# One GNN kernel on one core: the fixed one-hots read a kept column and stand ahead of the list load

## The reference

```python
x = _layernorm(x + _L0_gnn_ref(x, edge_index, ...))                # three SAGE layers
x = _layernorm(x + _L1_gnn_ref(x, edge_index, edge_attr_16, ...))  # one GIN layer with edge features
x = _layernorm(x + _L2_gnn_ref(x, edge_index, edge_weight, ...))   # two GCN layers
x = _layernorm(x + _L3_gnn_ref(x, ..., src, dst, edge_type_8))     # two RGCN layers, 8 relations
```

## Time and profile before

| | |
|---|---|
| three runs | 5378.65, 5391.27, 5395.21 us; median 5391.27 us |
| profiled execution | span 5394.1 us; no other time of it is given |
| PE busy | 4403.8 us, 82% |
| DVE busy | 3418.7 us, 63% |
| ACT busy | 2417.1 us, 45% |
| POOL busy | 1920.8 us, 36% |
| DMA | 815.61 MB, mean 151 GB/s |

### The profile page before, as it was taken

The page is one execution under the profiler, slowest core; times in us unless marked ns, Lnnn a source line. Parts: engine busy times, 40 slices in busy tenths (PEclk is TensorE's granted clock), DMA queues, the critical chain, the costliest instruction groups (busy, mean ns, idle before and its releaser), DMA issues.

```text
span 5394.1 us, 129622 instructions
## 1 busy us (share of the span) xinstructions
PE 4403.8 (82%) x25128; PEld 2883.3 (53%) x25129; DVE 3418.7 (63%) x10510; ACT 2417.1 (45%) x4969; POOL 1920.8 (36%) x1886
## 2 busy tenths in 40 slices
PE   6998997767878888867777588887799996888895
PEld 4664554333445555435554355544577773667772
DVE  5553454676545555448997688876466663777774
ACT  2442442554357777626664466664222221333332
POOL 5650782654033433116550434310433312333310
PEclk9999999898889999989999899998899999999998
DMA  4663884555334444326563466653444433444332
GB/s 142 217 210 116 267 270 142 182 182 176 99 117 148 146 151 145 113 88 174 174 172 105 143 203 212 203 177 108 145 136 136 136 120 103 133 122 133 116 111 76
DMA packets 443919, 815.61 MB, mean 151 GB/s; under 512 B 70872, under 2 KB 76818, under 8 KB 443828
## 3 DMA queue, kind: packets, MB, share of 16 engines
q1 hardware_dynamic: 389172, 697.28, 38.6%
q0 software_dynamic: 54656, 117.32, 9.1%
HBM read 480.10 MB, written 334.22 MB: 151 GB/s over the span
## 4 chain that ended last, share of the span: by engine, by line
PE 46%; issue 14%; DVE 12%; ACT 8%; DVEq 6%; POOL 5%; DMA 4%; ACTq 3%; SPq 1%; POOLq 0%
PE p_agg L1116 7%; PE p_edge L1103 7%; PE p_agg L1118 6%; PE p_tr L1103 6%; PE p_agg L1149 5%; POOL raw L680 4%; DVE onehot L1550 4%; DMA h_in<-feature 3%; DVE stats L1640 3%; ACT o L881 2%; ACT u L900 2%; PE p_wide L1236 2%; PE p_agg L1142 2%; PE p_dense L1192 2%; PE p_dense L1168 2%
## 5 line engine op out<-in xcount | busy, mean ns | idle before, releaser
L1550 DVE TENSOR_SCALAR onehot<-iota,dst_f,negbase 128x512 f16<-128x512 f16 (+1 forms) x2848 | 1110.7, 444 | 823.8 <-PE p_agg L1149 304.8
L1116 PE MATMUL p_agg<-onehot,msg 128*128 128x512 f16 (+1 forms) x2848 | 1135.9, 399 | 584.9 <-DVE onehot L1550 325.1
L680 POOL DMA_INDIRECT raw<-node_s,src_i x980 | 958.1, 978 | 1462.8 <-DMA node_s<-o 560.6
L1118 PE MATMUL p_agg<-onehot,msg 128*128 128x512 f16 (+1 forms) x2848 | 1135.7, 399 | 0.0
L1116 PEld LDWEIGHTS p_agg<-onehot,msg 128*128 x2848 | 281.7, 99 | 930.7 <-issue 780.8
L680 POOL DMA_INDIRECT raw<-node_x,src_i x392 | 378.2, 965 | 553.3 <-DMA feature<-more_masked 253.7
L1149 PE MATMUL p_agg<-h_in,w 128*128 128x512 f32 x784 | 442.5, 648 | 110.6 <-DMA h_in<-feature 109.4
L881 ACT ACTIVATE o<-v_ring,nmr,rstd 128x128 f32 (+1 forms) x1176 | 472.3, 483 | 60.0 <-DVE nmr L1656 55.3
L1640 DVE BATCH_NORM_STATS2 stats<-v_ring 128x6 f32 (+1 forms) x1960 | 417.5, 278 | 44.1 <-DVE v_ring L1630 14.7
L900 ACT ACTIVATE u<-v_ring,nmr,rstd 128x128 f32 (+1 forms) x784 | 312.4, 481 | 223.9 <-DVE res_in L1686 135.6
L1118 PEld LDWEIGHTS p_agg<-onehot,msg 128*128 x2848 | 282.9, 99 | 218.9 <-issue 33.1
(11 more groups left out here) (260 smaller groups left out, 7817.8 us busy)
## 6 DMA issues: line engine op xcount, KB each, us to landing
node_s<-o SPq DMA_DIRECT2D x392, 256.0 KB
h_in<-feature SPq DMA_DIRECT2D x392, 256.0 KB
feature<-u SPq DMA_DIRECT2D x294, 256.0 KB
node_x<-o SPq DMA_DIRECT2D x294, 256.0 KB
res_in<-node_x SPq DMA_DIRECT2D x294, 256.0 KB
h_in<-node_s SPq DMA_DIRECT2D x196, 256.0 KB
h_t<-dinv_scratch SPq DMA_DIRECT2D x196, 256.0 KB, 3.6
h_in<-in_x SPq DMA_DIRECT2D x98, 256.0 KB
```

The source lines that it names most:

```text
L680: nc.gpsimd.indirect_dma_start(out=raw[:, (e % RING) * BATCH + j, :], out_offset=None, in_=src_d, in_offset=bass.IndirectOffsetOnAxis(ap=s ...
L1116: nc.tensor.matmul(p_agg[:, a, :], tile_ap(msg, t, 0, D), oh, start=first, stop=True, skip_group_check=True)
L1118: return nc.tensor.matmul(p_agg[:, a, :], tile_ap(msg, t, D, 2 * D), oh, start=False, stop=True, skip_group_check=True)
L1550: return V.tensor_scalar(tile_ap(onehot, slot), iota[:, :], dst_f[:, bass.ds(t, 1)], negbase[:, bass.ds(it * 2 + a, 1)], ALU.subtract, ALU ...
```

## The change

Three things change, all in DVE's program.

1. A new SBUF tensor `place` of 128 x 294 f32 (98 halves x 3). In round 0, behind the three fixed compares of a half, DVE adds the tiles' `dst_f` columns and the half's `negbase` column into it. In the seven rounds after, `fixed_onehots` compares `iota` with one column of `place` (is_equal alone), with an address that hangs on the step's number and no longer on the list words.
2. In these rounds `next_items(it)` begins with `fixed_onehots(it + 1, 0)`; then come the list load, the batches of rounds 3, 6 and 7, and the further groups of half 1 of `it`. The load was first before. In `mean_step` the degrees of half 0 go ahead of all of it.
3. The tile number is shifted out of the word inside the If of `more_onehots`; the odd half's fixed one-hots (`odd_onehots`) need none after round 0.

```diff
+        place = sb("place", [P, NHALF * EVERY])
...
                 def first_onehots(it, a, t0):
 
-                    if k:
-                        wait(dve, q.out_done, it * 2 + (a - 1))
-                    elif rel:
-                        wait(dve, q.turned, it * 2 + (a - 1))
                     for j in range(EVERY):
                         last = compare(it, a, EVERY * a + j, (t0 + j).with_bounds(min_val=0, max_val=TILES - 1))
                     last.then_inc(q.every_ready.semaphore, 1)
+                    V.tensor_scalar(place[:, bass.ds((it * 2 + a) * EVERY, EVERY)],
+                                    dst_f[:, bass.ds(t0.with_bounds(min_val=0, max_val=TILES - EVERY), EVERY)],
+                                    negbase[:, bass.ds(it * 2 + a, 1)], None, ALU.add)
+
+                def fixed_onehots(it, a):
+
+                    wait(dve, q.out_done, it * 2 + (a - 1))
+                    for j in range(EVERY):
+                        last = V.tensor_scalar(tile_ap(onehot, EVERY * a + j), iota[:, :],
+                                               place[:, bass.ds((it * 2 + a) * EVERY + j, 1)], None, ALU.is_equal)
+                    last.then_inc(q.every_ready.semaphore, 1)
 
                 def more_onehots(it, a, these):
 
-                    t0, i0, i1 = these
+                    word, i0, i1 = these
                     with dve.If(i0 < i1):
+                        t0 = tile_in(dve, word)
                         with dve.Fori(i0, i1) as i:
...
+                    if k:
+                        fixed_onehots(it + 1, 0)
+                    first, second, third = packed(words[0:1, bass.ds(it * 2 + 1, 3)], PT)
+                    ahead = None
                     if rel or k == 3:
-                        these, (now, after) = odd_list(dve, PT, it * 2 + 1)
-                        if rel:
-                            first_onehots(it + 1, 0, after[0])
-                        each_batch(dve, *these, batch)
-                        ahead = None
+                        each_batch(dve, batch_in_word(dve, second), batch_in_word(dve, first), batch)
                     elif exists(it + 2):
-                        (e0, e1, e2), (now, after) = later_list(dve, PT, it * 2 + 1)
+                        e1, e2 = batch_in_word(dve, first), batch_in_word(dve, third)
                         if is_zero(it):
-                            each_batch(dve, e0, e1, batch)
+                            each_batch(dve, batch_in_word(dve, second), e1, batch)
                         ahead = (e1, e2)
-                    else:
-                        now, after = pair_list(dve, PT, it * 2 + 1)[0]
-                        ahead = None
-                    more_onehots(it, 1, now)
-                    return after[:3], after[3], ahead
+                    i1 = group_of(dve, second)
+                    more_onehots(it, 1, (first, group_of(dve, first), i1))
+                    return (second, i1, group_of(dve, third)), third, ahead
 
                 def onehots(it, these):
 
-                    if not rel:
-                        first_onehots(it, 0, these[0])
+                    if not k:
+                        first_onehots(it, 0, tile_in(dve, these[0]))
                     more_onehots(it, 0, these)
+
+                def odd_onehots(it, third):
+
+                    if k:
+                        fixed_onehots(it, 1)
+                    else:
+                        first_onehots(it, 1, tile_in(dve, third))
...
                 def mean_step(it):
+                    degrees(it, 0)
                     now, after, ahead = next_items(it)
-                    degrees(it, 0)
...
                 if r:
                     wait(dve, S[r - 1].out_done, NHALF)
-                now, after = pair_list(dve, PT, 0)[0]
-                first_onehots(0, 0, now[0])
-                first_onehots(0, 1, after[0])
+                first, second = packed(words[0:1, 0:2], PT)
+                if k:
+                    fixed_onehots(0, 0)
+                    fixed_onehots(0, 1)
+                else:
+                    first_onehots(0, 0, tile_in(dve, first))
+                    first_onehots(0, 1, tile_in(dve, second))
```

## The result

The changed kernel is slower: 5414.56 us, median of 5 runs (5401.09 to 5425.77), against 5388.94 us for the kernel before (5 runs, 5378.65 to 5395.21). The ratio is 1.0047, with a 95% interval of 1.0032 to 1.0062. The profiled execution took 5414.56 us, with a span of 5412.8 us, so it stands at the median. Predicted were 5360 us and a range from 5312 to 5396. One of the ten executions of run 2 took 7058 us at a granted clock of 0.58, and counts in no ratio.

The account below looks back on a forecast made before the run. No single engine was taken to bound the kernel; DVE was on the path in rounds 4 and 5. Terms of 28 and 21 us won less 18 lost gave 31 us less: 5360 us, range 5312 to 5396.

Parts of the forecast that it names:

- Place columns: Round 0: 196 adds on DVE, 55 us as upper bound, hidden under 191 us of waiting for PE; cost nothing.
- Shorter compares: 2058 fixed compares on DVE read one column in place of two: 50 ns off each, bounds 0 and 65.
- Rival 1: One column less saves nothing in the fixed compares: 19 of the 31 us go, about 5379 us; chance 0.16.
- Register work: DVE's odd half: two register additions for the tile number fall away, 0.15 us a step in round 5.
- The list load behind the compares: Even half, rounds 4 and 5: 0.17 us won a step, 5 and 8 us; whole term 21 us.
- early one-hots in round 4: One-hots for half 0 come earlier where PE is on the path: 5 us, between 0 and 20.
- Added wait: List load and groups stand behind out_done of half 0: 1 us late per odd half with groups, 18 us lost.
- it can win only where DVE is on the path: The change edits DVE's program alone; rounds 4 and 5, the GCN layers, were named as such rounds.
- Neither wait has a one-hot in it: Round 3's loop: ACT idles 3.45 us for DVE's edge_v, DVE 3.59 us for ACT's msg.
- rival 2: Early one-hots free PE: its round 3 waits, 53 us, vanish; rounds 4 and 5 win more; about 5307 us; chance 0.12.
- Rival 3: Wait dearer than win: load begins only after the third compare starts, odd groups late; 35 us more, 5426; chance 0.12.
- theory A: Stated for the experiments, not the prediction: earlier one-hots merge PE's short waits into long ones and cost clock.

Follow-up runs that it names:

- run 2: Changed kernel, but fixed compares ahead of the list load in rounds 4 and 5 alone, load first elsewhere; 5375.66 us, 0.9969 of the kernel before.
- run 6: Changed kernel with load first everywhere and a second column of zeros in the compares from the kept column; 5381.15 us, 0.9971 of the kernel before.
- Run 1: Changed kernel with the list load ahead of the fixed compares again in every round, kept columns staying; 5368.38 us, 0.9963 of the kernel before.
- run 4: Changed kernel, but in round 3 the order is load, fixed compares, batch; 5410.27 us, 1.004 of the kernel before.
- run 9: Changed kernel, but in round 3 two fixed compares stand ahead of the load, the third behind the batch; one execution, 5393.87 us.

## Why the prediction was wrong

**Place columns: right.** They cost nothing: round 1's first closing product stands at 541.0 us, after 540.6 before.

**Shorter compares: right, and a little small.** 60 ns by the medians, where I took 50 between 0 and 65. Rival 1 is out. In rounds 4 and 5 the column brought 17.3 us by run 6, where rival 1 would have lost 13.

**Register work: right in kind, too small.** The sum had 0.15 us at the odd half, 7 us in round 5, and hid it in round 4. Run 6 against the kernel before leaves 10.5 us for it in round 5 and 3 to 10 in round 4, since it fell away at the even half as well.

**The list load behind the compares: the wait moved as I said, and the gain was 0.** I had 0.17 us a step, 13 us for both rounds, and 5 for early one-hots in round 4. DVE's timeline of round 5, before, from the batch's operation to the multiply:

```profile
3401.25 1.08 DVE L1545 TENSOR_TENSOR msg<-raw,msg  x1
3403.20 1.13 DVE L1550 TENSOR_SCALAR onehot<-iota,dst_f,negbase 128x512 f16<-128x512 f16 x3 [0.86 <-issue]
3404.24 0.68 DVE L1667 TENSOR_TENSOR agg_t<-p_agg,h_t 128x512 f32<-128x512 f32 x1
```

The change:

```profile
3405.39 1.08 DVE L1546 TENSOR_TENSOR msg<-raw,msg  x1
3406.39 0.87 DVE L1567 TENSOR_SCALAR onehot<-iota,place 128x512 f16<-128x512 f16 x3
3408.12 0.69 DVE L1682 TENSOR_TENSOR agg_t<-p_agg,h_t 128x512 f32<-128x512 f32 x1 [0.86 <-issue]
```

Run 1, the load first:

```profile
3374.89 1.08 DVE L1546 TENSOR_TENSOR msg<-raw,msg  x1
3376.64 0.93 DVE L1567 TENSOR_SCALAR onehot<-iota,place 128x512 f16<-128x512 f16 x3 [0.68 <-issue]
3377.61 0.69 DVE L1686 TENSOR_TENSOR agg_t<-p_agg,h_t 128x512 f32<-128x512 f32 x1
```

The idle time did move from ahead of the compares to ahead of the multiply, 0.86 us each, as predicted. From the batch's operation to the multiply it is 2.99 us before, 2.73 with the change, and 2.72 with the load first. The 0.26 us belong to the shorter compare and the missing register work at the even half, which my sum had counted at the odd half alone; the order adds nothing. So the two rounds' total came out near by luck (33 us for some 38, or 26 against the second profile of the kernel before), by wrong shares.

**Added wait: right in round 1.** "1 us late per odd half with groups", 8 us: round 1 lost 8.2. The timelines of PE and DVE there, after, answer to the earlier trace rows:

```profile
855.20 0.39 PE L1117 MATMUL p_agg<-onehot,msg 128*128 x1 [1.40 <-DVE onehot L1551]
...
853.87 0.73 DVE L1551 TENSOR_SCALAR onehot<-iota,dst_f,negbase 128x512 f16 x2 [1.32 <-issue]
```

PE waits 1.40 us before the group, where it waited 0.31. With the load first round 1 was back. Round 6 lost 4.0 of an expected 7, and got it back with the load first too.

**Rounds 3 and 7: the step that failed.** It is the step from "it can win only where DVE is on the path" to a sum in which earlier one-hots cost PE nothing elsewhere. "Neither wait has a one-hot in it" was right of the loop in round 3: ACT's wait for edge_v did not shorten (3.45 us before, 3.44 and 4.32 in two steps after), and rival 2's 53 us did not come. What I left out is what PE does with one-hots that come sooner into a wait that does not end sooner. I let PE idle at no cost. In fact the idle time moved behind the one-hot products, joined the wait that stood there, and brought the clock to the level of 1.2 GHz for products on the path: 19.5 us in round 3 and 17.1 in round 7, together more than the 33 us won. Rival 3 had the sign, and with 5426 us nearly the time, but by luck. By its reason rounds 4 and 5 would have lost 26 us, and they won; in these two rounds the list loads began ahead of the third compare; and run 4 took the load from behind the compares and round 3 stayed.

**Round 2** lost 5.0 us. With round 7 I had it at 7 us won and 3 lost. With kept columns in it, it took 553.0 to 563.1 us; with the compares of before 544.7 to 549.9. Of its 196 closing matmuls 49 take over 0.8 us in the change and 38 before, which fits theory A. No run was made for round 2 alone, and kernels alike in it differ by 7 us, so that stays argued.

## What to carry to other kernels

Where an operand is made sooner for an engine that then waits for something else, ask where its idle time goes: two short waits with work between them can become one long one, and on PE the long one can be paid again in the products behind it. Compare PE's busy time for the same number of matmuls, stretch by stretch, and where it grew look at the granted clock. Then make an operand sooner only in the stages whose end hangs on it: with the load first, kept columns in rounds 3 to 6 alone gave 0.9%, in all rounds 0.4%. A change to one engine's program has to be priced on the engines that it frees as well.

## What the runs showed of the hardware

A second per-partition column costs the f16 compare of 512 columns 60 ns (348 and 408 ns, medians), more than the 49 ns of the 128-column rows. The formula of the Trainium skill (VectorE: DVE Perf Modes, section The TRN2 errata) has no term for columns, so by it nothing would have been saved. The measurement decides against it.

The closing product in round 7 ran at the level of 1.2 GHz behind a wait of 3.18 us, and came slow behind one of 2.57 us too (run 1: 1.95 us at 4906.83); behind 1.84 and 1.47 us it did not. The length of the last wait alone does not decide it: in the changed kernel the clock fell behind a wait of 1.87 us (closing product at 4641.00, 0.66 over 5 us) and stayed at 1.00 behind one of 3.02 us (at 4895.61). More work for PE (six matmuls, overwritten) made the work behind them faster: 1.12 us in place of 2.07.

A list load on DVE takes 0.75 us (median). In round 3 of the changed kernel 16 of 49 took 1.22 to 1.46 us. The compares ahead of it are not the cause: with the load ahead of them (run 4) 15 of 49 were as long, up to 1.52 us, and behind two compares (run 9) none was over 0.77. In rounds 4 and 5 the change's loads stayed under 0.77 us. What lengthened the others stays open.
